# Attention groups started one step before the last one ends, and the correction row D of the next group moved to the maxima's banks

## Chip, core and metric

The kernel runs on one core of one Trainium2 chip. The metric is the device time of one execution in microseconds. The time before is the median of three executions, 1124.32 us (1123.53 to 1124.39).

## The reference, cut to what is computed

```python
xn = _layernorm(x)                       # x: (2, 1024, 512)
qkv = clip(xn @ Wqkv.T, -8, 8)           # q, k, v; q and k then get a layer norm with weights
scores = einsum('bqhd,bkhd->bhqk', q, k) * 16 ** -0.5      # 32 heads of 16
scores = scores + slopes[None, :, None, None] * rel         # ALiBi
scores = where(causal, scores, -1e30)
out = einsum('bhqk,bkhd->bqhd', softmax(scores), v) @ Wout.T
g = silu(ffn(xn))                        # gated FFN with 4-bit weights, inner size 1792
return x + out * g
```

## The kernel before

There are three stages. The first (to about 186 us in the profile) makes q, k and v, splits q and k into three bf16 parts each and writes them to HBM as `stk`. The second (to about 714 us), the one that is changed, is attention. The third is the FFN and the output.

The second stage works on 16 **groups** (NG = 16, index i): 2 batches times 8 groups of 4 heads (GH = 4). A group has 1024 queries and 1024 keys. It is done in 12 **steps** (NSTEP = 12, index e): a step takes one half of the queries (512) against one tile of 128 keys, eight steps for the upper half of the queries and then four (FIRST = 8) for the lower half. In a step

- `second(i, s, e, p)`, p = 0 and 1, computes on TensorE the scores of two heads into the PSUM tile `pair[p]`, on the diagonal with two more matmuls that add the mask (`behind`). It waits until the exponential has read that pair (`exp_done`);
- ScalarE takes the exponential of each pair, 128x1024 where the step is full, into `pr` (`exps`);
- `pv(i, s, e-1)` multiplies the exponentials of the step before with the values into `bank[3]` (`b_o`).

No maximum is subtracted in ScalarE. The row maximum comes in as rows of the operand: **D0** (lower half of the queries) and **D1** (upper half) are the negated maxima, split into three bf16 parts by five small operations on GpSimd (`chain`), transposed on TensorE (`trans_d`), copied to SBUF (`dt_sb`) and written by a 12 KB DMA from ScalarE's queue (`send_d`) into rows 108 to 110 of the operand `qs`. The first scores of group i+1 wait for D1's DMA (`d1_in`).

The maxima need the scores in the other orientation. These **pieces** (query tile, head, first key, width; 48 in a group) go through a ring of three PSUM banks `b_m`: TensorE fills a bank (`score`), VectorE reads its maximum (`take`; with the causal mask and one more small instruction where the piece ends on the diagonal, `tensor_reduce` where not) and frees it (`m_free`). A piece waits until the one three places before it is read. In group i the pieces of query tiles 2 and 3 are the group's own (`OWN`), all others belong to group i+1. `plan` says which pieces stand after which of the 36 **places** (step e, parts 0, 1, 2: after `second(…, 0)`, after `second(…, 1)`, after `pv`). The ring also carries the outputs: `copy_o` (ScalarE) copies `b_o` to `ot`, `trans_o` transposes it in four matmuls, VectorE divides (`normalise`); O1 is the upper half of the queries, O0 the lower.

At the end of a group the order before is: D1's transpose into `pair[0]` after step 10, ScalarE's copy of it, step 11's scores, `pv` of step 10, four pieces, `pv` of step 11, two pieces, O0, and then the next group.

SP's queue loads the operands of group i+2 in two halves of 14 or 15 DMAs (`load(..., 1)` after `pv` of step 7, `load(..., 0)` with the values after `pv` of step 11), and before them 4-bit weights for the third stage (`half_job`: `zst` and `sst`, 448 KB each), which ScalarE converts (`convert`, two instructions) and GpSimd subtracts (`job`). Three such jobs lie in two groups.

Of the kernel before, what the change touches and what calls it, by code (L numbers as in the profile page):

```python
# [18 lines left out]

# [7 lines left out]
BF16 = mybir.dt.bfloat16  # L27
# [31 lines left out]
def build(nc, x, wproj, lnw, w_all, z_all, s_all, ident_in, identb_in, tri_in, behind_in, qrows, krows, out):  # L59
# [7 lines left out]
    with ExitStack() as ctx:  # L67
# [142 lines left out]
        LATER_KEYS = len(EARLY) // 2  # L210

        PLACES = 3 * NSTEP
        OWN_END = 8
        LOW_AT = 15
        EARLY_END = 28
        TAIL = 6
        BEFORE = 4
        D0_AT, D1_AT, O1_AT = 5, 10, 9
        JOB_AT = 6

        def spread(lot, lo, hi):

            width = [w for e in range(NSTEP) for w in (512 - STEPS[e][2], 512 - STEPS[e][2], 512 - STEPS[e - 1][2])]
            total, work = sum(width[lo:hi]), sum(pc[3] + 60 for pc in lot)
            out, at, passed = {h: [] for h in range(PLACES)}, 0, 0
            for h in range(lo, hi):
                passed += width[h]
                while at < len(lot) and (h == hi - 1 or sum(pc[3] + 60 for pc in lot[:at]) < work * passed / total):
                    out[h].append(lot[at])
                    at += 1  # L230
            return out
        parts_of_plan = (spread(LATE[HEAD:], 0, OWN_END), spread(EARLY[:LATER_KEYS], OWN_END - 1, LOW_AT),
                         spread(EARLY[LATER_KEYS:], LOW_AT, EARLY_END), spread(LATE[:HEAD - TAIL], EARLY_END, PLACES))
        plan = {h: sum((part[h] for part in parts_of_plan), []) for h in range(PLACES)}
        plan[3 * D0_AT + 2].append("D0")
        plan[3 * O1_AT + 2].append("O1")
        tail = LATE[HEAD - TAIL:HEAD] + ["O0"]

        own = [x for h in range(PLACES) for x in plan[h] if x in LATE[HEAD:] or isinstance(x, str)] + ["O0"]
        order = [x for h in range(PLACES) for x in plan[h]] + tail  # L240
        RING = len(order)
        assert RING % 3 == 0
        HEAD_ORDER = LATE[:HEAD // 2] + EARLY + LATE[HEAD // 2:HEAD]
        PREP = len(HEAD_ORDER)
        number = ({x: n for n, x in enumerate(order)}, {x: n for n, x in enumerate(own)})

        def at(x, last):

            return number[last is True][x]

        def ring_bank(x, last):
            return b_m[(PREP + at(x, last)) % 3]

        def base(i):

            return PREP + RING * i

# [527 lines left out]
        USES = (NSTEP + 1, NSTEP)  # L785
        D1_USE = D1_AT + 1
# [3 lines left out]
        def full(i, e, p, last):  # L790

            return USES[p] * i + e + 1 + (1 + (e > D1_AT and not last) if p == 0 else 0)

        def full_d1(i):

            return USES[0] * i + D1_USE + 2

# [5 lines left out]
        with nc.Block() as block:  # L803
            @block.sync
            def _(sp):
# [16 lines left out]
                def body(i, s, ip, last):  # L822
# [20 lines left out]
            def _(pool):  # L843
# [16 lines left out]
                def body(i, s, ip, last):  # L860

                    pool.wait_ge(m_free, base(i) + at(LATE[-1], last) + 1)
                    pool.wait_ge(s_full[0], USES[0] * i + 1)
                    chain(pool, mx0[:, :, :], 2 * i + 1)
                    job(ip, (0, 2)[s])
                    if not last:

                        pool.wait_ge(mx1_done, i + 2)

                        pool.wait_ge(m_full, base(i) + at("D0", last) + 1)  # L870
                        chain(pool, mx1[:, 0, :, :], 2 * i + 2)
# [823 lines left out]
```

## Time and profile before

| | |
|---|---|
| median of three executions | 1124.32 us |
| the profiled execution's own time | 1123.91 us |
| its span, first to last instruction | 1121.8 us |
| mean granted TensorE clock | 0.993 of full speed |
| busy share of the span, TensorE / VectorE / ScalarE / GpSimd | 93% / 83% / 65% / 41% |
| second stage, groups 1 to 14, 226.22 to 685.79 us | 459.57 us, of which TensorE busy 433.28 |

A busy TensorE is not one at its peak: the records of matmuls overlap, and a short wait can hide in them. In the timelines below the start times are therefore what is read: what lies between the starts of two rows is what the first took, waits included.

### The profile page before, as it was taken

Reading aid. Unit: us, or ns where it says so; the run is one execution under the profiler, and the core shown is the slowest. Engines: PE = TensorE matmul, PEld = TensorE weight load, DVE = VectorE, ACT = ScalarE, POOL = GpSimd, SP = SyncE. Lnnn points to the kernel's source line nnn. Section 1 sums busy time; section 2 is a strip of 40 time slices with the busy share of each in tenths; the row PEclk is TensorE's granted clock in tenths of the full one; section 3 lists DMA queues with packets and bytes.
Section 4 is the critical chain, followed back from the end, with each engine's and each line's share of the span. In section 5 each row is a group of like instructions: output and inputs, shape, how many; then the busy total and the mean of one; then the engine's idle time right before and its main releaser. Section 6 shows DMA issues by size and latency. Waiting matters only on the chain. (4 is left out here: it accounts for less than half of the span.)

```text
span 1121.8 us, 18965 instructions
## 1 busy us (share of the span) xinstructions
PE 1043.7 (93%) x6242; PEld 635.6 (57%) x6242; DVE 926.4 (83%) x2147; ACT 725.7 (65%) x1167; POOL 465.1 (41%) x554
## 2 busy tenths in 40 slices
PE   5999987999999999999999999899999999999995
PEld 4788764333333433333333333487778778777874
DVE  6788897787878888788888875579989998998896
ACT  3666565676667667666666667567747766774774
POOL 2666645111111111111111111039946864994786
PEclk9999998999999999999999999999999999999998
DMA  6254753453543334454343433100120011012001
GB/s 212 77 155 142 214 144 94 133 119 72 142 108 95 113 100 119 75 142 109 89 120 96 120 77 105 39 1 0 39 70 7 1 55 59 1 39 75 1 1 38
DMA packets 98584, 95.32 MB, mean 85 GB/s; under 512 B 28030, under 2 KB 80950, under 8 KB 98486
## 3 DMA queue, kind: packets, MB, share of 16 engines
q1 hardware_dynamic: 96854, 93.72, 29.9%
q8 instruction: 50, 0.82, 0.3%
q10 hardware_dynamic: 1632, 0.39, 0.2%
q14 instruction: 48, 0.39, 0.1%
HBM read 72.45 MB, written 21.23 MB: 84 GB/s over the span
## 5 line engine op out<-in xcount | busy, mean ns | idle before, releaser
L883 ACT ACTIVATE pr<-pair 128x1024 f32<-128x1024 f32 (+3 forms) x384 | 293.1, 811 | 151.2 <-PE pair L999 97.0
L266 DVE CUSTOM_DVE_ANT_0 bank<-bank,sg 128x384 f32<-128x384 f32 (+1 forms) x488 | 227.5, 521 | 65.6 <-PE bank L276 62.1
L1527 PE MATMUL pair<-xc_lo,w_gu 128*128 128x512 f32 x448 | 181.5, 405 | 4.5 <-DVE xc_lo L1363 4.5
L1528 PE MATMUL pair<-xc_hi,w_gu 128*128 128x512 f32 x448 | 175.3, 391 | 0.0
L269 DVE TENSOR_REDUCE mx<-bank 128x1 f32<-128x512 f32 x240 | 150.1, 682 | 8.9 <-PE bank L276 8.2
L1375 DVE SCALAR_TENSOR_TENSOR gate<-pair,sgu,gate 128x512 f32<-128x512 f32 x168 | 124.5, 741 | 25.7 <-PE pair L1528 24.1
L1166 POOL TENSOR_TENSOR yt<-yt,tmp 128x512 f32<-128x512 f32 x96 | 124.2, 1314 | 0.0
L276 PE MATMUL bank<-ks,qs 108*128 108x512 bf16 (+3 forms) x384 | 107.7, 329 | 5.3 <-DVE mx L266 5.1
L1527 PEld LDWEIGHTS pair<-xc_lo,w_gu 128*128 128x128 f32 x448 | 84.1, 188 | 37.3 <-DVE up L1375 6.6
L1156 POOL TENSOR_TENSOR h_lo<-gate,h_hi 128x512 fp32r<-128x512 f32 x56 | 72.5, 1296 | 76.6 <-ACT h_hi L1209 76.6
L994 PE MATMUL pair<-s_sb,xin_c 111*128 111x512 bf16 (+3 forms) x384 | 95.1, 332 | 7.7 <-ACT dt L395 2.9
L276 PE MATMUL bank<-xin_c,s_sb 108*128 108x512 bf16 (+3 forms) x344 | 98.0, 334 | 4.4 <-DVE mx L266 4.1
L994 PE MATMUL pair<-qs,ks 111*128 111x512 bf16 (+3 forms) x384 | 93.1, 327 | 7.5 <-ACT pr L883 4.7
L1540 PE MATMUL bank<-h_lo,w_d 128*128 128x512 f32 x224 | 89.7, 400 | 2.9 <-POOL h_lo L1156 2.2
L1528 PEld LDWEIGHTS pair<-xc_hi,w_gu 128*128 128x128 f32 x448 | 84.3, 188 | 13.6
L371 POOL TENSOR_SCALAR dneg<-mx 128x16 f32<-128x16 f32 x32 | 8.2, 255 | 198.0 <-DVE mx L266 113.2
L850 POOL TENSOR_TENSOR w_gu<-sst,zst 128x896 fp32r<-128x896 f32 x16 | 33.4, 2085 | 135.5 <-ACT zst L896 135.5
L1541 PE MATMUL bank<-h_hi,w_d 128*128 128x512 f32 x224 | 88.2, 394 | 0.0
L709 PE MATMUL bank<-wq_hi,xt_lo 128*128 128x512 f32 x192 | 79.4, 413 | 5.4 <-DVE xt_lo L597 5.4
L1241 ACT ACTIVATE gate<-gate 128x512 f32<-128x512 f32 x56 | 35.4, 632 | 73.2 <-DVE gate L1375 73.2
L1166 POOL TENSOR_TENSOR yt<-yt,oin_v 128x512 f32<-128x512 f32 x48 | 65.3, 1360 | 37.9 <-ACT oin_v L1263 37.5
L1009 PE MATMUL bank<-pr,oin_v 128*17 128x512 f32 (+3 forms) x768 | 80.8, 492 | 0.0
(125 smaller groups left out, 2121.4 us busy)
## 6 DMA issues: line engine op xcount, KB each, us to landing
stk<-parts SPq DMA_DIRECT2D x16, 768.0 KB, 5.7
zst<-in_z_all SPq DMA_DIRECT2D x24, 448.0 KB, 4.0
sst<-in_w_all SPq DMA_DIRECT2D x24, 448.0 KB, 4.7
xin_c<-in_x SPq DMA_DIRECT2D x32, 256.0 KB, 3.3
s_sb<-stk SPq DMA_DIRECT2D x96, 64.0 KB
xin_c<-stk SPq DMA_DIRECT2D x96, 64.0 KB
qs<-stk SPq DMA_DIRECT2D x96, 64.0 KB
ks<-stk SPq DMA_DIRECT2D x96, 64.0 KB
```

What stands on the lines that cost most here:

```text
L266: dve.tensor_tensor_reduce(out=src, in0=src, in1=tri[:, 512 - w:512], scale=1.0, scalar=-3.0e38, op0=ALU.add, op1=ALU.max, accum_out=dst). ...
L269: dve.tensor_reduce(dst, src, AX.X, ALU.max).then_inc(m_free, 1)
L276: pe.matmul(b[:, 0:w], qs[s][0:ROWS_MAX, qt // 4, j, (qt % 4) * P:(qt % 4 + 1) * P], ks[s][0:ROWS_MAX, j, k0:k0 + w], start=True, stop=Tru ...
L883: act.activation(pr[e % 3][:, 2 * p:2 * p + 2, 0:w], pair[p][:, :, 0:w], ACT.Exp, scale=SCALE)\
L994: mm = pe.matmul(pair[p][:, jj, 0:512 - c0], ks[s][0:ROWS, j, kt * P:(kt + 1) * P], qs[s][0:ROWS, qb, j, c0:512], start=True, stop=not dia ...
L1009: mm = pe.matmul(b_o[32 * j:32 * j + VW, c0:512], vs[s][:, kt, j * VW:(j + 1) * VW], pr[e % 3][:, j, 0:512 - c0], start=(kt == 0), stop=(k ...
L1166: pool.tensor_tensor(yt[t][:, :], yt[t][:, :], tmp[n % 3], ALU.add).then_inc(dn_pool, 1)
L1375: dve.scalar_tensor_tensor(out=a, in0=GB[j % 4], scalar=scale_of(n, k, it), in1=a, op0=ALU.mult, op1=ALU.add)\
L1527: pe.matmul(GB[j % 4], w, xc_lo[:, k, :], start=True, stop=False)
L1528: pe.matmul(GB[j % 4], w, xc_hi[:, k, :], start=False, stop=True).then_inc(gu_done, 1)
L1540: pe.matmul(y[t][:, :], w_down(it, t), h_lo[n % 4][:, :], start=True, stop=False)
L1541: pe.matmul(y[t][:, :], w_down(it, t), h_hi[n % 4][:, :], start=False, stop=True).then_inc(dn_done, 1)
```

## The change

The scores keep their places and their order; the plan is now written out as a table of 36 places. What differs in the second stage:

- `pv` of step 11 and O0 of group i move into group i+1: `pv` to step 0 (part 2), O0 to step 1 (part 1). All six last pieces stand together at the end of the group. `copy_o(i, 1)` follows the exponentials of step 0 of group i+1.
- D1 is transposed into a ring bank and copied by VectorE; before, it went into `pair[0]` and was copied by ScalarE, and step 11 waited for the copy.
- `second` of a group's first step now waits for the exponentials of the last step of the group before.
- On SP, `load(..., 1)` waits for the scores of step 7 and not for `pv` of step 7; `load(..., 0)` for the scores of step 11, and the values' DMA alone for `pv` of step 11.
- The job that stood at the end of an even group (`convert(ip, 1)`) comes before the exponentials of step 2 of the odd one.

```diff
+        PLAN = (
+            "2 2", "2", "",
+            "2 3", "O0 3", "3",
...
+            "7", "0", "O1",
+            "", "0", "D1",
+            "", "", "0 0 1 1 1 1",
+        )
...
-                        sp.wait_ge(pv_done, PV0 + NSTEP * i + FIRST)
+                        sp.wait_ge(s_full[1], full(i, FIRST - 1, 1))
                         load(sp, i + 2, s, 1)
 
+                        sp.wait_ge(s_full[1], full(i, NSTEP - 1, 1))
+                        load(sp, i + 2, s, 0, values=False)
+
                         sp.wait_ge(pv_done, PV0 + NSTEP * i + NSTEP)
-                        load(sp, i + 2, s, 0)
+                        load_v(sp, i + 2, s)
...
-                        if e == D1_AT + 1 and not last:
-                            send_d1(act, 1 - s, full_d1(i), i + 2, pair[0][:, 0, :])
+                        if e == place_of["D1"] + 1 and not last:
+
+                            act.wait_ge(m_free, number(i, "D1") + 1)
+                            send_d(act, 1 - s, 1, d1_in)
+                        if e == JOB1_AT and s == 1:
+                            convert(ip, 1)
...
+                        exps(i, e, 0)
+                        exps(i, e, 1)
+                        if e == 0 and i > 0:
+                            copy_o(i - 1, 1)
+                        if e == FIRST:
                             copy_o(i, 0)
...
+                    if x in ("D0", "D1"):
+                        dve.wait_ge(m_full, n + 1)
+                        dve.tensor_copy(dt_sb[int(x[1])][:, :], ring_bank(i, x)[0:48, 0:P // 2].bitcast(BF16)).then_inc(m_free, 1)
...
+                    if i > 0 or e > 0:
+
+                        pe.wait_ge(exp_done, 2 * NSTEP * i + 2 * e - 1 + p)
...
-                            if h == 3 * e + 2 and e > 0:
+                            if part == 2 and e > 0:
                                 pv(i, s, e - 1)
...
-                        if e == NSTEP - 1:
-                            ring(i, s, tail[:BEFORE], last)
-                        if e == D1_AT and not last:
-
-                            pe.wait_ge(exp_done, 2 * NSTEP * i + 2 * e + 1)
-                            trans_d(pe, 2 * i + 2, pair[0][:, 0, :], s_full[0])
-                    pv(i, s, NSTEP - 1)
-                    ring(i, s, tail[BEFORE:], last)
+                            elif part == 2 and i > 0:
+                                pv(i - 1, 1 - s, NSTEP - 1)
+                            for x in plan[3 * e + part]:
+                                if present(x, i):
+                                    fill(i, s, x)
```

Below is TensorE's order at D1, in the first group (slot 0, operands `s_sb` and `xin_c`), before the change. `d3` is the split maximum, `identb` the identity, `pair` the score tiles, `bank3` the output's accumulator.

```order
L384 MATMUL pair0<-identb,d3 48x128 [waits d_chain,exp_done]
L994 MATMUL pair0<-s_sb,xin_c 128x128 [waits d_copied]
L994 MATMUL pair0<-s_sb,xin_c 128x128
L999 MATMUL pair0<-behind,identb 128x128 x2
L994 MATMUL pair1<-s_sb,xin_c 128x128 [waits exp_done]
L994 MATMUL pair1<-s_sb,xin_c 128x128
L999 MATMUL pair1<-behind,identb 128x128 x2
```

And with the change:

```order
L397 MATMUL bank0<-identb,d3 48x128 [waits d_chain,m_free]
L1012 MATMUL pair0<-s_sb,xin_c 128x128 [waits exp_done]
L1012 MATMUL pair0<-s_sb,xin_c 128x128
L1017 MATMUL pair0<-behind,identb 128x128 x2
L1012 MATMUL pair1<-s_sb,xin_c 128x128 [waits exp_done]
L1012 MATMUL pair1<-s_sb,xin_c 128x128
L1017 MATMUL pair1<-behind,identb 128x128 x2
```

D1 now goes into a ring bank and waits for the ring (`m_free`), and step 11's first scores wait for an exponential and no longer for the copy of D1. The second place is the end of the group on TensorE, from the fourth of the six last pieces to the first scores of the next group (`qs1`, `ks1`), before:

```order
L276 MATMUL bank0<-ks1,qs1 128x256 [waits m_free]
L1009 MATMUL bank3<-pr2,oin_v 17x128 [waits exp_done]
L1009 MATMUL bank3<-pr2,oin_v 17x128 x3
L276 MATMUL bank1<-ks1,qs1 128x256 [waits m_free]
L276 MATMUL bank2<-ks1,qs1 128x256 [waits m_free]
L1018 MATMUL bank0<-ident,ot 128x128 [waits ot_done,m_free]
L1018 MATMUL bank0<-ident,ot 128x128 x3
L994 MATMUL pair0<-qs1,ks1 128x512 [waits d1_in]
L994 MATMUL pair0<-qs1,ks1 128x512
```

With the change, from the same piece to `pv` of step 11:

```order
L289 MATMUL bank1<-ks1,qs1 128x256 [waits m_free]
L289 MATMUL bank2<-ks1,qs1 128x256 [waits m_free]
L289 MATMUL bank0<-ks1,qs1 128x256 [waits m_free]
L1012 MATMUL pair0<-qs1,ks1 128x512 [waits exp_done,d1_in]
L1012 MATMUL pair0<-qs1,ks1 128x512
L289 MATMUL bank1<-ks1,qs1 128x384 [waits m_free]
L289 MATMUL bank2<-ks1,qs1 128x384 [waits m_free]
L1012 MATMUL pair1<-qs1,ks1 128x512 [waits exp_done]
L1012 MATMUL pair1<-qs1,ks1 128x512
L289 MATMUL bank0<-ks1,qs1 128x384 [waits m_free]
L1027 MATMUL bank3<-pr2,oin_v 17x128 [waits exp_done]
L1027 MATMUL bank3<-pr2,oin_v 17x128 x3
```

The `pv` of 17x128 (step 11's) and the transposes of `ot` have left the way to the first scores; the `pv` stands now behind the third piece of step 0, and O0 (not shown) behind the second scores of step 1. On ScalarE the same stretch reads before:

```order
L395 ACTIVATE dt1<-pair0 48x128 [waits s_full0]
L389 DMA qs1<-dt1 3x16x128 [waits d_copied]
L883 ACTIVATE pr2<-pair0 128x2x128 [waits pv_done,s_full0]
L883 ACTIVATE pr2<-pair1 128x2x128 [waits pv_done,s_full1]
L890 ACTIVATE ot<-bank3 128x512 [waits pv_done]
L895 ACTIVATE sst<-sst 128x896 [waits z_in]
L896 ACTIVATE zst<-zst 128x896
```

and with the change:

```order
L402 DMA qs1<-dt1 3x16x128 [waits m_free]
L896 ACTIVATE pr2<-pair0 128x2x128 [waits pv_done,s_full0]
L896 ACTIVATE pr2<-pair1 128x2x128 [waits pv_done,s_full1]
L896 ACTIVATE pr0<-pair0 128x1024 [waits pv_done,s_full0]
L896 ACTIVATE pr0<-pair1 128x1024 [waits pv_done,s_full1]
L903 ACTIVATE ot<-bank3 128x512 [waits pv_done]
L896 ACTIVATE pr1<-pair0 128x1024 [waits pv_done,s_full0]
```

The copy of D1 is gone from ScalarE, its DMA waits for VectorE (`m_free`), and the copy of the output stands behind the exponentials of the next group's first step.

## Rows read from the trace of the kernel before

**Rows 1.** Busy time by engine in stretches: one group, and the sum of groups 1 to 14.
```profile
391.00:423.54 32.54, 30.87 (x236) 12.59 (x234) 26.71 (x86) 21.75 (x30) 4.26 (x11) 1.00 0.37 96
...
sum 459.57, PE 433.28 PEld 175.98 DVE 374.69 ACT 306.79 POOL 74.16; mean PE 30.95 PEld 12.57 DVE 26.76 ACT 21.91 POOL 5.30
```
**Rows 2.** Waits, 226 to 686 us: us in total, times, longest.
```profile
PE pair L994 <- ACT dt L395: 5.1, 14, 0.4
...
PEld pair L994 <- DMA s_sb<-dt: 1.4, 3, 0.9
...
PEld pair L994 <- DMA qs<-dt: 0.6, 2, 0.3
```
**Rows 3.** Timeline of TensorE around the starts of groups 4 (325.56) and 7 (423.54).
```profile
325.56 0.61 PE L994 MATMUL pair<-s_sb,xin_c 111*128 111x512 bf16 x2 [0.66 <-DMA s_sb<-dt]
...
419.25 0.24 PE L384 MATMUL pair<-identb,d 128*48 128x128 bf16 x1
...
421.85 0.41 PE L1009 MATMUL bank<-pr,oin_v 128*17 128x128 f32 x8
422.20 0.39 PE L276 MATMUL bank<-ks,qs 108*128 108x256 bf16 x2
423.07 0.63 PE L1018 MATMUL bank<-ident,ot 128*128 128x128 f32 x4 [0.49 <-DVE mx L266]
423.54 0.60 PE L994 MATMUL pair<-qs,ks 111*128 111x512 bf16 x2
...
425.58 0.60 PE L994 MATMUL pair<-qs,ks 111*128 111x512 bf16 x2 [0.52 <-ACT pr L883]
...
428.89 0.38 PE L276 MATMUL bank<-ks,qs 108*128 108x512 bf16 x1
...
430.83 1.05 PE L1009 MATMUL bank<-pr,vs 128*17 128x512 f32 x8
```
**Rows 4.** Timeline of ScalarE at the same two starts; ACTq is its queue.
```profile
321.01 0.73 ACTq L389 DMA_DIRECT2D s_sb<-dt  x1
...
419.82 0.73 ACTq L389 DMA_DIRECT2D qs<-dt  x1
...
422.33 0.60 ACT L890 ACTIVATE ot<-bank 128x512 f32<-128x512 f32 x1 [1.03 <-PE bank L1009]
...
424.51 3.75 ACT L883 ACTIVATE pr<-pair 128x1024 f32<-128x1024 f32 x4
```
**Rows 5.** Timeline of VectorE in the first steps of group 7.
```profile
423.74 0.26 DVE L929 RECIPROCAL rec<-bank 128x16 f32<-128x16 f32 x1 [0.35 <-PE bank L1018]
...
424.38 0.56 DVE L266 CUSTOM_DVE_ANT_0 bank<-bank,sg 128x384 f32<-128x384 f32 x1
...
429.31 0.70 DVE L266 CUSTOM_DVE_ANT_0 bank<-bank,sg 128x512 f32<-128x512 f32 x1
```
**Rows 6.** Timeline of TensorE in the first steps of group 6, an even one.
```profile
391.00 0.60 PE L994 MATMUL pair<-s_sb,xin_c 111*128 111x512 bf16 x2
...
392.71 0.60 PE L994 MATMUL pair<-s_sb,xin_c 111*128 111x512 bf16 x2 [0.19 <-ACT pr L883]
...
397.97 1.05 PE L1009 MATMUL bank<-pr,oin_v 128*17 128x512 f32 x8
```
**Rows 7.** Timeline of SP's queue in group 7.
```profile
415.05 0.33 SPq L180 DMA_DIRECT2D s_sb<-stk  x1
...
422.55 0.82 SPq L180 DMA_DIRECT2D s_sb<-stk  x1
...
444.11 0.33 SPq L811 DMA_DIRECT2D zst<-in_z_all  x1
...
447.92 0.33 SPq L180 DMA_DIRECT2D qs<-stk  x1
```
**Rows 8.** The page's DMA issues: KB each, median us from issue to landing.
```profile
sst<-in_w_all SPq DMA_DIRECT2D x24, 448.0 KB, 4.7
...
out<-s_sb SPq DMA_DIRECT2D x16, 256.0 KB, 2.5
```

More of the change, by code:

```diff
@@ L20 @@
+from collections import Counter
 from contextlib import ExitStack
@@ L209, in build @@
         HEAD = 8
[L210 to L239, printed above, removed]
@@ L240, in build @@
-        order = [x for h in range(PLACES) for x in plan[h]] + tail
-        RING = len(order)
-        assert RING % 3 == 0
+        OWN = LATE[HEAD:]
         HEAD_ORDER = LATE[:HEAD // 2] + EARLY + LATE[HEAD // 2:HEAD]
         PREP = len(HEAD_ORDER)
[L245 to L256, printed above, removed]
+        PLACES = 3 * NSTEP
@@ new lines, in build @@
+        plan = [[item(token) for token in row.split()] for row in PLAN]
+        in_order = [x for row in plan for x in row]
+        assert sorted(x for x in in_order if not isinstance(x, str)) == sorted(EARLY + LATE)
+        place_of = {x: h // 3 for h, row in enumerate(plan) for x in row}
+        of_kind = {name: [x for x in in_order if x in lot] for name, lot in
+                   (("own", OWN), ("early", EARLY), ("head", LATE[:HEAD]),
+                    ("upper", [x for x in EARLY if x[2]]), ("lower", [x for x in EARLY + LATE[:HEAD] if not x[2]]))}
@@ new lines, in build, with present, number @@
+        JOB_AT, JOB1_AT = 6, 2
+        def present(x, i):
+            if x == "O0":
+                return i > 0
+            if x in ("D0", "O1") or x in OWN:
+                return True
+            return i < NG - 1
+        ring_of = [[x for x in in_order if present(x, i)] for i in range(NG)]
+        ring_of[NG - 1].append("last O0")
+        place_in = [{x: n for n, x in enumerate(r)} for r in ring_of]
+        first_in = [PREP + sum(len(r) for r in ring_of[:i]) for i in range(NG)]
+        def number(i, x):
+            return first_in[i] + place_in[i][x]
@@ L258, in take, with ring_bank @@
+        def ring_bank(i, x):
+            return b_m[number(i, x) % 3]
         def take(dve, pc, b, n):
@@ L783, in w_half, with full @@
             return w_d[:, ip * HALF:(ip + 1) * HALF] if n == 2 else w_gu[:, (2 * ip + n) * HALF:(2 * ip + n + 1) * HALF]
-        USES = (NSTEP + 1, NSTEP)
-        D1_USE = D1_AT + 1
         EXTRA = 1
         PV0 = 3
[L790 to L796, printed above, removed]
+        def full(i, e, p):
+            return NSTEP * i + e + 1 + (p == 0)
         def groups(body):
@@ L981, in slot0_free, with fill @@
-                def slot0_free(i, e, last):
-                    if e == D1_AT + 1 and not last:
-                        pe.wait_ge(d_copied, i + 2)
-                    elif e > 0:
-                        pe.wait_ge(exp_done, 2 * NSTEP * i + 2 * e - 1)
+                def fill(i, s, x):
+                    n = number(i, x)
+                    if x in ("D0", "D1"):
+                        pe.wait_ge(m_free, n - 2)
+                        trans_d(pe, 2 * i + (1, 2)[int(x[1])], ring_bank(i, x), m_full)
+                    elif x == "O1":
+                        trans_o(i, 0, n)
+                    elif x == "O0":
+                        trans_o(i - 1, 1, n)
+                    elif x in OWN:
+                        score(pe, s, x, ring_bank(i, x), n)
+                    else:
+                        if x == of_kind["upper"][0]:
+                            pe.wait_ge(stk_in[1 - s][1], LOADS[1] * (i // 2 + 1 + s))
+                        if x == of_kind["lower"][0]:
+                            pe.wait_ge(stk_in[1 - s][0], LOADS[0] * (i // 2 + 1 + s))
+                        score(pe, 1 - s, x, ring_bank(i, x), n)
```

121 lines of the change are left out of this document (59 added, 62 removed).

## Prediction

> **What bounds the kernel now.** I read the busy time of stretches first. From the start of group 1 to the start of group 15, 14 groups take 459.6 us, 32.8 us each, and TensorE is busy in 31.0 of them, VectorE in 26.8, ScalarE in 21.9 [rows 1]. TensorE bounds the stage, but its records overlap, so the 1.8 us left is not all that it waits. I therefore went on to the timelines and read distances between starts. The end of a group is where the change works. The marks there are D1's transpose (419.25) and the first scores of the next group (423.54): 4.29 us apart [rows 3]. In them stand step 11's scores, `pv` of step 10, six pieces, `pv` of step 11 and O0. Two waits are seen: the wait for ScalarE's copy of D1, 5.1 us in 14 groups or 0.36 each [rows 2], and 0.49 before O0, which comes last there [rows 3].
>
> The row to look at next is one that does not look like a bound. D1's DMA is issued at 419.82 and the scores that need it start at 423.54, 3.72 later, and they are released by O0's transposes and not by the DMA [rows 3, 4]. But in group 4 the issue is at 321.01 and the start at 325.56, 4.55 later, and there it is the DMA that ends the wait, after 0.66 us [rows 3, 4]. The weight loads of such scores waited for D1's DMA in five of the 15 starts, 1.4 + 0.6 = 2.0 us in all [rows 2]. So the DMA's landing lies just below the work that covers it in ten starts, and above it in five. A mean start is thus 4.29 + 2.0/15 = 4.42 us behind D1.
>
> **The change, part by part.** I cut a period of 32.8 us into three stretches: D1 to the next group's first scores (a), these to `pv` of step 0 behind the four narrow pieces, which is step 2's last part (b), and the rest (c).
>
> *The rest (c)* keeps its instructions and their order: the pieces stand at the same places as before (the two orders of TensorE agree there piece by piece), so nothing is gained by the order of keys and width itself. D1's copy adds 0.2 us to VectorE where it is idle. Zero, while VectorE has 6 us of 32.8 free [rows 1].
>
> *Stretch (a), what TensorE has to do.* Before, the last pieces are issued by 422.20 + 0.39 = 422.59, which is 3.34 behind D1. Of that 0.36 (the copy of D1) and 0.35 (`pv` of step 11, 421.85 to 422.20) go [rows 2, 3]. TensorE is ready for the next group 2.6 us behind D1, where it was 4.29. If nothing else held it, 1.7 us would be won each time.
>
> *Stretch (a), what D1 needs.* The DMA is still issued 0.57 behind D1 (419.25 to 419.82): VectorE's copy takes the place of ScalarE's, and I add 0.01 for it, 0.58 [rows 3, 4]. Then it has to land, L, and 0.05 passes until the scores start (an estimate from the small distance at a semaphore). Neither end of L is shown directly, so I bound it. From below by the shortest landing of the page, 2.5 us for the output's stores, at a time with little other traffic [rows 8]. From above by group 4, 4.5 us [rows 3, 4]. Now L lies under 3.7 in ten starts and between 3.7 and 4.5 in five; I take its mean as 3.6. So with the change the first scores come max(2.6, 0.63 + L) behind D1, and since 0.63 + 2.5 is already 3.1, D1's DMA sets it in every case. The cover of 3.72 us that hid the landing is what the change takes away: the wait that goes at O0 comes back as a wait for `d1_in`.
>
> *What becomes of L.* It is longer than 2.5 because SP's loads are in flight. Before, the load of the second half starts at 415.05, 4.8 us before D1's DMA, and runs to 422.55, where the next load follows without a gap [rows 7]. With the change it starts when step 7's scores are done, which is about when SP has issued the two weight DMAs (444.11, and the second some 1.1 later), so at about 445.2 in place of 447.92 [rows 7]. Its 14 DMAs take 7.5 us (415.05 to 422.55), and D1's DMA at 452.7 comes just when they have been issued and the next load begins. That is for a smaller L. Against it: 0.9 MB of weights, which take 4.7 us to land [rows 8], now stand directly ahead of these loads, where 3.4 us lay between. I take 3.3.
>
> The Trainium skill ("DMA: Bandwidth & Descriptors", "Queues, rings and completion order") says that a DMA's semaphore increment is a strongly ordered write, which lands only after every earlier write of that DMA engine, across its queues. By it D1's landing hangs on what SP has in flight and not on D1's 12 KB, and stays slow as long as loads run beside it. Group 4 agrees with it but doesn't prove it.
>
> *Stretch (b).* It now holds `pv` of step 11 and O0 as well, 0.35 + 0.5 us of TensorE. Count from the first scores (0). The first exponential ends so that step 1's scores start at 1.71 in group 6, behind a seen wait of 0.19 [rows 6]; in group 7, where ScalarE converts weights first, at 2.04 [rows 3]. TensorE would be there at 1.36: the second scores start at 0.76 and take 0.44, the third piece some 0.16 (an estimate: 384 of 512 columns of the 0.22 below). `pv` of step 11, 0.35, fills this gap exactly: 1.71. Step 1's second scores follow at 2.63 (the second exponential, 3.75/4 later [rows 4]). Then ScalarE copies the output, 0.60 long [rows 4], so O0 starts at about 3.2. VectorE reads it 0.67 later (423.07 to 423.74) and goes on to a piece 1.31 behind O0's start [rows 3, 5], at 4.5. TensorE goes on at 3.7: a piece 0.22 (428.89 to the next scores), `pv` 0.99, a piece, scores 0.44; the fourth 512-wide piece is issued at 5.55 and read 0.42 later (428.89, 429.31), at 5.97 [rows 3, 5]. Before, that reading was 429.31 - 423.54 = 5.77 behind the first scores, and the `pv` that ends the stretch started 1.52 behind it, at 7.29 (430.83); in group 6 at 397.97 - 391.00 = 6.97 [rows 3, 5, 6]. With the change 5.97 + 1.52 = 7.49, against a mean of 7.13: +0.36.
>
> **The sum.** For a start with loads: 0.63 + L - 4.42 + 0.36 = L - 3.43. With L = 3.3, -0.13 us, in 14 starts -1.8. The 15th start (group 15) has no loads beside it: 0.63 + 2.5 - 4.29 + 0.36 = -0.8. Together -2.6 us. The profiled execution took 1123.91 us (span 1121.8), 0.4 under the median, so 1121.3 for it and 1121.7 for the median: -0.2%.
>
> **The rivals.**
> 1. *D1's DMA stays as slow as it is* (the skill's rule, with the loads beside it as before): L = 3.6 gives +0.17 x 14 - 0.8 = +1.6 us, 1125.9. For it: SP issues without a pause before and after. Chance 0.25.
> 2. *The landing gets worse*, the other side: the loads come directly behind 0.9 MB of weights, the queue is still full when D1's DMA is issued, and every start is like group 4's, L = 4.5: +1.07 x 14 - 0.8 = +14 us, 1138. It decides from L = 3.7 on. For it: such a start exists. Against: 7.5 us have passed since the weights' issue, and they take 4.7. Chance 0.22.
> 3. *D1's DMA meets a quiet moment*, L = 2.5: -0.93 x 14 - 0.8 = -14 us, 1110. For it: the gap between the two loads. Against: SP hardly pauses. Chance 0.20.
> 4. *The wait for D1 is no bound at all* and all of 1.7 - 0.36 = 1.3 us is won 15 times: -20 us, 1104. It needs a landing under 2.0 us, below any row. Chance 0.02.
>
> **How the numbers follow.** The forecast (L from 3.0 to 3.6, 1117 to 1126) has 0.31. My sum of stretch (b) may be off by 0.2 us a group, 3 us in all. The range runs from 1110 to 1134 (L = 2.5 to 4.2). A measurement of this kernel tells 0.2%, 2.2 us, from no change, so faster is under 1122.1: half of the forecast's case, all of 3 and 4, a part of 1, together 0.43; within 0.2% 0.29; slower, 2 and the rest of 1, 0.28.
>
> **What would show it.** In the profile after: the wait for the copy of D1 and the waits before O0 at the end of a group are gone; in their place the first scores of nearly every group wait for the DMA of `dt`, 0.5 to 1.5 us; D1 to the first scores takes 3.9 us (L = 3.3), and the first scores to the `pv` of step 0 7.5. ScalarE's conversion in step 2 costs nothing. The prediction is wrong if the first scores do not wait for `dt`, if L is under 3 or over 3.7, or if a wait for exponentials appears in steps 1 to 3 where ScalarE has the output's copy and the conversion.

## The result and the profile after

Over 20 executions of each kernel the median is 1131.51 us (1125.89 to 1143.0) against 1124.14 us (1123.11 to 1128.68): a ratio of 1.007, with a 95% interval of 1.0055 to 1.0085. The changed kernel is 0.7% slower, where 0.2% faster was forecast. The profiled execution took 1139.53 us, its span is 1137.7, so it is one of the longer ones of the 20. Its mean granted clock of TensorE is 0.977. In the others it lies between 0.971 (the two of 1142.03 and 1143.0 us) and 0.986 (one of them of 1127.49), always under the 0.993 of the profile before. The kernel before is not at 0.993 each time either: 22 more executions of it, taken beside the first experiments, have 0.986 to 0.994.

The page of the changed kernel: the span, the busy times by engine, and the granted clock in 40 slices.

```profile
span 1137.7 us, 18980 instructions
...
PE 1058.1 (93%) x6242; PEld 639.5 (56%) x6242; DVE 930.1 (82%) x2162; ACT 722.3 (63%) x1152; POOL 465.4 (41%) x554
...
PEclk9999999999999998999999999999999999999997
```

TensorE is busy 14 us longer than before (1043.7) at the same instructions. The waits of TensorE in the second stage (us in total, times, longest), to be laid beside [rows 2]:

```profile
PE pair L1012 <- DMA qs<-dt: 10.8, 7, 3.0
PE bank L289 <- DVE mx L279: 8.3, 28, 0.3
PE pair L1012 <- DMA s_sb<-dt: 7.5, 7, 1.9
```

The wait for ScalarE's copy is gone. In its place 14 of the 15 starts show a wait for D1's DMA, 18.3 us in all. The start of group 7 on TensorE, with [rows 3] beside it (columns as there: start, us, instructions, idle time before and what ended it):

```profile
425.85 0.24 PE L397 MATMUL bank<-identb,d 128*48 128x128 bf16 x1
...
427.81 0.91 PE L289 MATMUL bank<-ks,qs 108*128 108x256 bf16 x3 [0.29 <-DVE mx L279]
431.16 1.04 PE L1012 MATMUL pair<-qs,ks 111*128 111x512 bf16 x2 [2.43 <-DMA qs<-dt]
431.99 0.85 PE L289 MATMUL bank<-ks,qs 108*128 108x384 bf16 x2
432.62 1.06 PE L1012 MATMUL pair<-qs,ks 111*128 111x512 bf16 x2
433.48 0.53 PE L289 MATMUL bank<-ks,qs 108*128 108x384 bf16 x1
433.94 0.63 PE L1027 MATMUL bank<-pr,oin_v 128*17 128x128 f32 x8
434.50 1.03 PE L1012 MATMUL pair<-qs,ks 111*128 111x512 bf16 x2
...
436.67 0.60 PE L1038 MATMUL bank<-ident,ot 128*128 128x128 f32 x4
...
438.63 0.60 PE L1012 MATMUL pair<-qs,ks 111*128 111x512 bf16 x2
```

D1 at 425.85, the next group's first scores at 431.16: 5.31 us, before 4.29. The reader should then look at a column that the prediction never read, the duration: scores of the same shape take 0.60 us each in [rows 3], 1.04 to 1.06 here, and 0.60 again from 438.63 on. Group 11, some 140 us later, has the same rows with a shorter wait and the old durations:

```profile
568.83 0.61 PE L1012 MATMUL pair<-qs,ks 111*128 111x512 bf16 x2 [0.47 <-DMA qs<-dt]
...
569.60 0.60 PE L1012 MATMUL pair<-qs,ks 111*128 111x512 bf16 x2
...
570.29 0.41 PE L1027 MATMUL bank<-pr,oin_v 128*17 128x128 f32 x8
570.63 0.61 PE L1012 MATMUL pair<-qs,ks 111*128 111x512 bf16 x2
...
572.04 0.63 PE L1038 MATMUL bank<-ident,ot 128*128 128x128 f32 x4
...
576.41 0.62 PE L1027 MATMUL bank<-pr,vs 128*17 128x512 f32 x4
...
```

The windows tell why. First three short stretches around the start of group 7, then the whole groups 1, 7 and 11 (columns: from:to, length, busy time of PE, PEld, DVE, ACT, POOL, then the granted clock, the DMA share and GB/s; the full clock, 2.4 GHz, is 1.00, and 0.50 is the lower level, 1.2 GHz):

```profile
427.00:430.40 3.40, 1.34 (x10) 0.46 (x6) 2.13 (x12) 0.66 (x2) 0.00 (x0) 0.88 1.15 142
431.10:434.50 3.40, 3.34 (x16) 1.05 (x16) 1.60 (x5) 1.80 (x2) 0.00 (x0) 0.50 0.85 127
434.50:437.90 3.40, 3.40 (x23) 1.43 (x19) 2.00 (x8) 2.79 (x5) 0.00 (x0) 0.72 0.54 124
...
224.01:258.12 34.11, 32.41 (x234) 13.02 (x235) 27.09 (x87) 22.65 (x30) 6.30 (x12) 0.95 0.51 115
...
431.16:465.84 34.68, 33.28 (x234) 13.25 (x235) 26.99 (x87) 22.64 (x30) 6.30 (x12) 0.92 0.50 112
568.83:601.03 32.20, 31.02 (x234) 12.54 (x234) 27.01 (x88) 22.31 (x30) 6.32 (x12) 1.00 0.50 122
```

In the first steps of group 7 TensorE is granted half its clock, after it had done nothing from 428.72, where its last piece ends, to 431.16. Its busy time grows by 2.3 us from group 11 to group 7 at the same 234 matmuls.

The table has the distances of all starts, taken from the traces: L is D1's DMA from its issue to the last update of its semaphore; a, from D1's transpose to the next group's first scores; rest, from a group's first scores to its D1. "Low" marks the groups in whose first steps the granted clock is 0.50.

```
                  before                 after
group i    L    a    rest of i+1    L    a    rest of i+1   low
 0        3.57  4.30   28.57       3.33  3.90   30.26       x
 1        3.89  4.51   28.27       3.28  3.85   30.26       x
 2        3.47  4.30   28.57       3.34  3.91   30.26       x
 3        4.50  5.12   28.26       4.22  4.79   30.21       x
 4        3.12  4.30   28.58       3.43  4.00   30.17       x
 5        2.69  4.30   28.25       3.40  3.97   30.17       x
 6        3.35  4.30   28.57       4.74  5.31   31.13       x
 7        3.46  4.29   28.25       2.98  3.55   28.86
 8        3.94  4.56   28.32       5.33  5.90   30.25       x
 9        3.74  4.36   28.57       3.80  4.37   30.26       x
10        3.92  4.54   28.33       2.77  3.34   28.87
11        3.86  4.48   28.26       2.77  3.34   28.86
12        3.60  4.30   28.58       4.07  4.63   30.21       x
13        3.38  4.29   28.26       3.23  3.80   30.22       x
14        2.21  4.29               2.29  2.86
```

The sum of the 14 periods from group 1's start to group 15's went from 459.57 to 477.61, +18.0 us, in three parts: the distances a −4.3; the rest of the undisturbed groups from 28.40 to 28.86, 14 x 0.46 = +6.4; and the low clock, 1.3 to 1.4 us in ten groups and 2.3 in group 7 (31.13 − 28.86), together +15.9. Group 1 starts 2.2 us earlier (226.22 and 224.01), and what follows the start of group 15 takes 436.1 us, 436.0 before. +18.0 − 2.2 = +15.8, against 15.9 between the spans.

The 2.2 us are no gain of the change. They are the low clock too, but in the kernel before, in the first steps of its first group (the second row is the changed kernel's):

```profile
191.23 1.04 PE L994 MATMUL pair<-s_sb,xin_c 111*128 111x512 bf16 x2 [2.71 <-DVE bank L955]
...
191.62 0.61 PE L1012 MATMUL pair<-s_sb,xin_c 111*128 111x512 bf16 x2 [2.71 <-DVE bank L972]
```

Behind the same idle time of 2.71 us the granted clock from 191.2 to 197.2 is 0.50 in the profile before and 1.00 in the one after. From its first scores to D1 the group takes 30.69 us before and 28.49 after. Without the low clock in either kernel, the changed one would still be 6.4 − 4.3 = 2.1 us slower (an estimate from these parts).

### The profile page after: what moved, and what is told of

It is laid out like the page before. It is cut to its first block and busy times, and to the rows that moved or that the text cites. A ratio compares the mean times of both kernels' runs of the same rounds, so it can differ in the third digit from the quotient of the medians.

```text
span 1137.7 us, 18980 instructions
## 1 busy us (share of the span) xinstructions
PE 1058.1 (93%) x6242; PEld 639.5 (56%) x6242; DVE 930.1 (82%) x2162; ACT 722.3 (63%) x1152; POOL 465.4 (41%) x554
## 5 line engine op out<-in xcount | busy, mean ns | idle before, releaser
L896 ACT ACTIVATE pr<-pair 128x1024 f32<-128x1024 f32 (+3 forms) x384 | 296.4, 811 | 190.0 <-PE pair L1017 101.3
L289 PE MATMUL bank<-ks,qs 108*128 108x512 bf16 (+3 forms) x384 | 112.8, 341 | 5.8 <-DVE mx L279 4.7
L1012 PE MATMUL pair<-qs,ks 111*128 111x512 bf16 (+3 forms) x384 | 99.2, 344 | 12.9 <-DMA qs<-dt 10.8
L1012 PE MATMUL pair<-s_sb,xin_c 111*128 111x512 bf16 (+3 forms) x384 | 97.8, 340 | 10.4 <-DMA s_sb<-dt 7.5
L289 PE MATMUL bank<-xin_c,s_sb 108*128 108x512 bf16 (+3 forms) x344 | 100.8, 339 | 5.3 <-DVE mx L279 4.3
L1027 PE MATMUL bank<-pr,vs 128*17 128x512 f32 (+3 forms) x768 | 81.6, 498 | 0.0
```

The costliest lines, as they stand in the source:

```text
L289: pe.matmul(b[:, 0:w], qs[s][0:ROWS_MAX, qt // 4, j, (qt % 4) * P:(qt % 4 + 1) * P], ks[s][0:ROWS_MAX, j, k0:k0 + w], start=True, stop=Tru ...
L896: act.activation(pr[e % 3][:, 2 * p:2 * p + 2, 0:w], pair[p][:, :, 0:w], ACT.Exp, scale=SCALE)\
L1012: mm = pe.matmul(pair[p][:, jj, 0:512 - c0], ks[s][0:ROWS, j, kt * P:(kt + 1) * P], qs[s][0:ROWS, qb, j, c0:512], start=True, stop=not dia ...
L1027: mm = pe.matmul(b_o[32 * j:32 * j + VW, c0:512], vs[s][:, kt, j * VW:(j + 1) * VW], pr[e % 3][:, j, 0:512 - c0], start=(kt == 0), stop=(k ...
```

## The experiments

Each ratio is against executions of the kernel before that were taken beside the run (medians 1124.0 to 1124.8 us). Averages and counts of groups are, unless said otherwise, over the 13 starts of groups 2 to 14 in the profiled execution. By that count the changed kernel has L = 3.64, a = 4.21 and ten groups with the low clock; the one before has 3.61, 4.43 and none.

**Without the loads.** Both kernels without the loads of groups 2 to 15, which then work with the data of groups 0 and 1 (the values too); the waits of the pieces for these loads are lowered to match, and everything else is kept. In the changed kernel (in the one before, its two load lines):

```diff
-                        load(sp, i + 2, s, 1)
...
-                        load(sp, i + 2, s, 0, values=False)
...
-                        load_v(sp, i + 2, s)
```

> The changed kernel without SP's loads of the operands of groups 2 to 15 (these groups then work on the data of groups 0 and 1; the weight DMAs stay). Theory A (D1's DMA lands late because SP's loads are in flight, that sets each group's start, and the wait lets TensorE's clock fall): D1's DMA lands in 2.2 to 2.3 us, the first scores come 2.9 us behind D1, the granted clock stays full in the stage, and the time is 1107 to 1111 us. Theory B (the stretch behind the start is what costs, by O0 and the later pieces, and the DMA is hidden): the time falls by no more than that of the kernel before without the loads, 1129 or more.

Measured: 1106.77 us (1105.96 to 1110.0), 0.9845 of the kernel before (0.9813 to 0.9877).

> The kernel before without SP's loads of the operands of groups 2 to 15 (same omission). Theory A: D1's DMA was hidden in ten of 15 starts, so only the late ones shrink to 4.29 us, -2 us in all: 1122. Theory B: the same, 1122 to 1124.

Measured: 1123.32 us (1120.63 to 1126.66), ratio 0.9987 (0.997 to 1.0005): no difference.

Two groups of the changed kernel without loads:

```profile
224.82:256.46 31.64, 30.91 (x235) 12.45 (x235) 26.91 (x88) 22.31 (x30) 6.31 (x12) 1.00 0.17 60
414.68:446.34 31.66, 30.93 (x236) 12.45 (x235) 26.93 (x90) 22.31 (x30) 6.31 (x12) 1.00 0.20 60
```

The starts of groups 1 to 15 now come 2.76 to 2.82 us behind D1, with landings of 2.2 us, and the granted clock is 1.00 in groups 1 to 14. In the kernel before, the landing falls to the same 2.2 us and the starts stay at 4.29 to 4.30: there the work in stretch (a) covers it. So the change does free 1.5 us a start (1106.77 against 1123.32 us where neither kernel has loads), and the landing of a 12 KB DMA beside the loads takes most of it back (a is 4.21 with them).

**The clock by itself.** Four matmuls of 512 columns that write into a ring bank whose next user overwrites them, between the last piece and the wait for `d1_in`. They add work and take no wait away.

```diff
+                        if e == 0 and i > 0:
+                            n = number(i, in_order[0])
+                            pe.wait_ge(m_free, n - 2)
+                            for _ in range(4):
+                                pe.matmul(b_m[n % 3][:, 0:512], ks[s][0:ROWS_MAX, 0, 0:P], qs[s][0:ROWS_MAX, 0, 0, 0:512], start=True, stop=True)
                         if e == 0:
                             pe.wait_ge(d1_in, 16 * i + 16)
```

> The changed kernel with four matmuls more per group (108x512 scores of the group's own, written to the ring bank that is filled next and overwritten there), between the last piece and the wait for D1's DMA: 0.86 us more of TensorE work where it would sit idle. Theory A (the idle time lowers the granted clock for the first steps of the group, which costs 1.4 us each time): no stretch at the lower clock at the starts of groups, 1124 to 1128 us, faster than the changed kernel though it does more. Theory B (the clock falls for another reason): 1131 or more.

Measured: 1128.62 us (1125.0 to 1134.68), ratio 1.0034 (1.0014 to 1.0053); the profiled span is 1123.5 us at a mean clock of 0.996. The start of a group, and the waits that are left:

```profile
389.86 1.04 PE L1050 MATMUL bank<-s_sb,xin_c 108*128 108x512 bf16 x4
390.73 0.60 PE L1012 MATMUL pair<-s_sb,xin_c 111*128 111x512 bf16 x2
...
391.50 0.59 PE L1012 MATMUL pair<-s_sb,xin_c 111*128 111x512 bf16 x2
```
```profile
PE pair L1012 <- DMA qs<-dt: 1.8, 2, 0.9
PE pair L1012 <- DMA s_sb<-dt: 0.2, 1, 0.2
```

The matmuls fill most of the time until the DMA lands, the scores behind them take 0.60 us, and no group of this execution has the low clock; a is 4.08 and the rest 28.86 on average. 14 us of span are back at the same instructions plus 60. The landings of this execution were shorter too (L = 3.20 on average), so part of the gain in a is theirs; the rest, 28.86 in every group, shows the clock by itself. Not every execution is as good (the median's is 3 us above the profiled one), but half of the loss goes with matmuls that compute nothing.

**The landing, by what SP has in flight.** The second load starts only when D1's DMA has landed:

```diff
                         sp.wait_ge(s_full[1], full(i, NSTEP - 1, 1))
+                        sp.wait_ge(d1_in, 16 * i + 32)
                         load(sp, i + 2, s, 0, values=False)
```

> The changed kernel, but SP's second load of a group waits until D1's DMA has landed. Theory A1 (what D1's landing waits for includes the loads issued behind it): it lands in 2.5 to 3.0 us in place of 3.6, the clock falls in few groups, 1112 to 1120 us. Theory A2 (it waits for what was issued ahead of it alone): it lands in 3.2 to 3.6 us, 1128 to 1132.

Measured: 1118.26 us (1116.11 to 1121.79), ratio 0.9946 (0.9926 to 0.9966). SP's queue between the two loads, with a gap from 417.96 to 420.74 where [rows 7] have none:

```profile
417.10 0.86 SPq L185 DMA_DIRECT2D xin_c<-in_krows  x1
420.74 0.33 SPq L181 DMA_DIRECT2D s_sb<-stk  x1
```

Issue to start falls from 3.69 to 3.00 on average (2.53 to 3.64), a to 3.52, and one group of 13 has the low clock. So the landing depends on the loads issued behind D1's DMA as well. The first load and the weights before it still stand ahead of D1's DMA; without any load issue to start is 2.26.

**The loads' waits alone, in both kernels.** The changed kernel with the waits of before, and the kernel before with the new ones:

```diff
-                        sp.wait_ge(s_full[1], full(i, FIRST - 1, 1))
+                        sp.wait_ge(pv_done, PV0 + NSTEP * i + FIRST)
                         load(sp, i + 2, s, 1)
-                        sp.wait_ge(s_full[1], full(i, NSTEP - 1, 1))
-                        load(sp, i + 2, s, 0, values=False)
                         sp.wait_ge(pv_done, PV0 + NSTEP * i + NSTEP)
-                        load_v(sp, i + 2, s)
+                        load(sp, i + 2, s, 0)
```

> The changed kernel with SP's loads back where they were (behind pv of step 7 and behind pv of step 11, values with the second). Theory A (the cover of D1's DMA is gone, and where the loads start makes no difference to its landing, 3.6 us in both): landing 3.5 to 3.8 us, time as the changed kernel's, 1128 to 1134 us. Theory C (the earlier loads, directly behind the weights, are what made the starts late): landings spread less and the time falls to 1120 to 1126.

Measured: 1139.49 us (1133.23 to 1146.9), ratio 1.0136 (1.009 to 1.0183). The expected 1128 to 1134 was missed. The landing is 3.5 on average, a 4.09, both a little under the changed kernel's, and 11 of 13 groups have the low clock. The profiled execution (1140.47) is as long as the changed kernel's (1139.53), so the trace does not show where the 8 us between the medians lie.

> The kernel before with only SP's loads started as in the changed one. Theory A: D1's DMA is covered for 3.72 us; a landing of 3.6 us in the mean with single ones over 4 costs 1 to 3 us in all, 1124 to 1127. Theory C: 1130 or more.

Measured: 1123.28 us (1121.58 to 1126.77), ratio 0.9993 (0.9982 to 1.0004). The landing falls from 3.6 to 3.1 on average, and a from 4.43 to 4.34 only. Next to nothing comes of it, because stretch (a) has 3.72 us of cover. The earlier loads are thus no part of the loss; they are harmless before and, by the medians, help after.

**D1 one place up**, so that the same cover stands behind an earlier issue:

```diff
-            "", "0", "D1",
+            "", "0 D1", "",
```

> The changed kernel with D1 transposed before pv of step 9 and not after it (one place earlier). Theory A: the DMA is issued about 0.5 us earlier against the rest of the group (ScalarE is busy with step 10 until then), the wait shrinks by that, and the clock falls in fewer groups: 1114 to 1124 us. Rival: GpSimd's split of the maxima is not ready so early, TensorE waits for it, and nothing is won: 1131.

Measured: 1123.58 us (1119.2 to 1132.22), ratio 0.9999 (0.9973 to 1.0025). The chain was ready in time. a is 4.22, counted from the earlier D1, and the rest is 28.1 in groups at the full clock: 32.3 us together, where the changed kernel has 4.21 + 28.86 = 33.1. Four of 13 groups have the low clock. That is a gain of 8 us on the changed kernel and none on the one before.

> Both: D1 one place earlier, and SP's second load behind D1's landing. Theory A: the two add, landing 2.9 us, start of the next group 0.5 us earlier than with the late load alone: 1109 to 1114 us. Rival: D1's DMA, issued earlier, stands deeper in the first load and lands 0.5 us later: 1116 to 1119.

Measured: 1116.97 us (1113.98 to 1122.79), ratio 0.9938 (0.9916 to 0.9959). That is 1.3 us under the late load alone, with intervals that overlap, so no difference is shown. The two gains do not add: issue to start is 3.48 here and 3.00 there. A reason would be that D1's DMA now goes out while more of the first load is in flight; no run separates it.

**An idle moment in the kernel before, first attempt.** D1 is sent behind step 11's exponentials instead of ahead of them.

```diff
...
+                    if not last:
+                        act.wait_ge(d_copied, i + 2)
+                        send_d(act, 1 - s, 1, d1_in)
```

> The kernel before, with D1's DMA issued on ScalarE behind the exponentials of step 11 (its copy stays where it was): about 1.5 us later, 2.1 us behind D1's transpose. No work is moved on TensorE. Theory A: with 3.6 us to land the first scores come 5.75 us behind D1 in place of 4.42, +1.3 us a group or +19 in 14; and the idle time of about 1.5 us lowers the clock, +1.4 us a group or +20: 1155 to 1165 us, with stretches at the lower clock at the starts of groups. Theory B (the lower clock belongs to something else of the changed kernel): 1143.

Measured: 1126.61 us (1124.28 to 1127.93), ratio 1.002 (1.0011 to 1.003). 1155 to 1165 was expected from an issue 1.5 us later. The issue moved by 0.70 us only, from 0.57 to 1.27 behind D1, and the landing was shorter (issue to start 3.27), so a is 4.54, TensorE is idle for 0.45 us at the most, and no group has the low clock. It tells nothing of the clock, since there was no longer wait to test it with.

**`pv` of step 11 back at the end of its own group**, in the changed kernel:

```diff
-                            elif part == 2 and i > 0:
-                                pv(i - 1, 1 - s, NSTEP - 1)
...
+                    pv(i, s, NSTEP - 1)
```

> The changed kernel with pv of step 11 back at the end of its own group; O0 stays in the next. TensorE then works 0.35 us of the wait for D1's DMA, and step 1's first scores wait for the exponential where the pv was. Theory A: the starts stay where they are, the wait is 0.35 us shorter, and the clock falls in fewer groups: 1124 to 1130 us. Rival: pv waits for the exponentials of step 11 and costs 0.3 us a group: 1131 to 1136.

Measured: 1127.8 us (1122.84 to 1132.46), ratio 1.0036 (1.0018 to 1.0055). The undisturbed rest stays 28.86, the shortest a is 3.16, and three of 13 groups have the low clock. `pv` costs nothing while TensorE waits for the DMA anyway and keeps it at work: the half of the overlap that moved it gained nothing.

**The weights late too.** Beside the late second load, the weights' DMAs that stood ahead of the first load go behind D1's landing; ScalarE converts them a step later.

```diff
-        JOB_AT, JOB1_AT = 6, 2
+        JOB_AT, JOB1_AT = 6, 3
...
-                    if not last:
+                    if not last and last is not None:
                         half_job(*((ip, 1), (ip + 1, 0))[s])
-                    else:
+                    elif last:
...
                         sp.wait_ge(s_full[1], full(i, FIRST - 1, 1))
                         load(sp, i + 2, s, 1)
 
+                        sp.wait_ge(d1_in, 16 * i + 32)
+                        half_job(*((ip, 1), (ip + 1, 0))[s])
                         sp.wait_ge(s_full[1], full(i, NSTEP - 1, 1))
                         load(sp, i + 2, s, 0, values=False)
```

> As the kernel with the second load behind D1's landing, and the weight DMAs that stood ahead of the first load moved behind that landing too (the conversion that follows first one step later). Theory A: the first load starts 1 us earlier and on free queues, D1's DMA lands in 2.3 to 2.7 us, 1108 to 1113 us. Rival: the second load comes 1 us later behind 0.9 MB and TensorE waits for it in step 5, or ScalarE for the weights in step 3: 1118 or more.

Measured: 1112.03 us (1110.84 to 1115.34), ratio 0.9899 (0.9881 to 0.9917), the shortest of all runs that keep their loads. SP and TensorE at the start of group 7, and two groups:

```profile
411.84 0.86 SPq L185 DMA_DIRECT2D xin_c<-in_krows  x1
415.41 0.37 SPq L818 DMA_DIRECT2D zst<-in_z_all  x1
```
```profile
412.58 0.24 PE L397 MATMUL bank<-identb,d 128*48 128x128 bf16 x1
...
415.44 0.60 PE L1014 MATMUL pair<-qs,ks 111*128 111x512 bf16 x2
```
```profile
225.07:257.04 31.97, 31.02 (x235) 12.46 (x235) 27.25 (x90) 22.42 (x30) 6.34 (x12) 1.00 0.60 125
415.44:447.08 31.64, 30.91 (x236) 12.53 (x235) 26.91 (x88) 22.44 (x30) 6.33 (x12) 1.00 0.52 126
```

SP issues nothing from 412.70 to 415.41, D1's DMA lands in that gap, issue to start is 2.40 on average (2.23 to 2.91), and at 415.44 the start comes 2.86 behind D1 and without an idle row. a is 2.92 on average, the rest 28.87, the clock 1.00. 14 x (2.92 + 28.87 − 32.83) = −14.6 us, and the 14 periods take 444.97, which is 14.6 less than before. The span is 11.0 less, because 4.7 us are lost behind the start of group 15 (440.7 us to the end, 436.0 before). There SP issues the last weights at 681.67 only, ScalarE waits for them, and TensorE for ScalarE:

```profile
687.34 0.95 ACT L910 ACTIVATE sst<-sst 128x896 f32<-128x896 int32 x1 [2.17 <-DMA sst<-in_w_all]
...
689.67 0.39 PE L1014 MATMUL pair<-qs,ks 111*128 111x128 bf16 x2 [2.92 <-ACT pr L898]
```

> The two together. Theory A: as with the weights late, within 2 us, since without a fallen clock it does not matter where pv of step 11 stands: 1107 to 1114.

Measured: 1116.52 us (1115.5 to 1118.35), ratio 0.9936 (0.9921 to 0.9951), 4.5 us slower than without `pv` there and outside the 1107 to 1114 expected. Once the DMA lands early, `pv` is what sets the start: a is 3.15 at the least. So the overlap is worth something, but only behind a fast landing.

**An idle moment in the kernel before, second attempt.** D1's DMA goes out behind ScalarE's copy of the output (its old place is taken out, as in the first attempt), then the same with nine matmuls of 512 columns in the place of the wait:

```diff
...
                     copy_o(i, 1)
+                    if not last:
+                        act.wait_ge(ot_done, EXTRA + 2 * i + 2)
+                        act.wait_ge(d_copied, i + 2)
+                        send_d(act, 1 - s, 1, d1_in)
```

> The kernel before with D1's DMA issued behind ScalarE's copy of the output, about 3.7 us behind D1's transpose in place of 0.57. The first scores then come 7.1 us behind D1 (landing 3.3), 2.7 us later than before, and TensorE is idle for that. Theory A (idle time lowers the clock): +2.7 x 15 = 40 us and in addition about 1.4 us a group at the lower clock, 1180 to 1190 us. Theory B (the clock falls by something of the changed order): 1160 to 1168 and the clock stays full.

Measured: 1184.93 us (1184.49 to 1190.14), ratio 1.053 (1.0505 to 1.0554). A start, and the windows around it:

```profile
418.01 1.03 PE L999 MATMUL pair<-s_sb,xin_c 111*128 111x512 bf16 x2 [2.53 <-DMA s_sb<-dt]
...
419.48 1.06 PE L999 MATMUL pair<-s_sb,xin_c 111*128 111x512 bf16 x2
...
424.91 0.60 PE L999 MATMUL pair<-s_sb,xin_c 111*128 111x512 bf16 x2
```
```profile
414.00:417.40 3.40, 0.99 (x10) 0.55 (x6) 1.85 (x8) 0.60 (x1) 0.00 (x0) 0.94 0.51 116
418.00:421.40 3.40, 3.39 (x9) 1.34 (x10) 1.65 (x6) 1.85 (x2) 0.00 (x0) 0.50 0.67 131
```

> The same with nine matmuls of 108x512 (1.9 us at the full clock) between the transposes of O0 and the wait for D1's DMA. Theory A: no fall of the clock at the starts, 1160 to 1168 us, faster than without them. Theory B: as without them.

Measured: 1157.18 us (1156.27 to 1159.59), ratio 1.0289 (1.0262 to 1.0316). A fourth execution took 5503.53 us; it is left out, and why it did is not known. A start of this one:

```profile
475.07 0.59 PE L999 MATMUL pair<-s_sb,xin_c 111*128 111x512 bf16 x2
...
476.03 0.60 PE L999 MATMUL pair<-s_sb,xin_c 111*128 111x512 bf16 x2 [0.19 <-ACT pr L884]
...
478.90 0.60 PE L999 MATMUL pair<-s_sb,xin_c 111*128 111x512 bf16 x2
```

Here the edits of the pair of kernels differ in nothing but idle or filled time: a is 6.79 and 6.64, the rest 30.49 and 28.29. With the wait all 13 groups have the low clock, the same 0.50 as in the changed kernel; filled, none, and the time is 27.8 us shorter at 135 matmuls more. So the order of work that the change brings is not needed for the low clock; the kernel before has it at every start once TensorE is idle there for 1.5 to 2.8 us.

## Why the prediction was wrong

The forecast was 0.2% faster, and the kernel became 0.7% slower; the time lies inside the range of 1110 to 1134 us, on the other side of the time before.

**What was right.** The bound that it named: D1's DMA sets every start, 0.05 us behind the landing, and the waits at the copy and at O0 at the end of a group are gone. Its issue, 0.58 behind D1 (0.52 measured). Stretch (b): 7.49 us forecast, 7.58 in group 11 (568.83 to 576.41) and in the other groups at the full clock, so +0.36 became +0.45. The conversion in step 2 and the order of the pieces cost and gain nothing. The start without loads (2.5 taken, 2.29 measured) and the L of before (3.6 taken as a mean, 3.61 measured; six of the 15 starts hung on it, not five).

**The first step that failed is the term L.** "I take 3.3": it was 3.62 on average over the 14 starts with loads (2.77 to 5.33), as before the change. In the sum it is worth 14 x 0.32 = +4.5 us. The argument for it was the place of the DMA between two loads. By the issues it does lie there (SP issues the first load's last DMA at 425.41 in group 6, D1's goes out at 426.37, the second load begins at 426.67), but the first load's semaphore is still being updated until 430.67, so both loads are in flight beside it. Rival 1, to which 0.25 was given, has the size right (3.6). The rule of the Trainium skill behind it ("DMA: Bandwidth & Descriptors", "Queues, rings and completion order": a completion is written only after the earlier writes of that DMA engine, across its queues) agrees with what the loads show: L is 2.2 us without them, 2.3 with 2.7 us of quiet on SP, 3.0 with the weights ahead, 3.6 with everything. Rival 1's sum gives 1125.9. The trace records the packets of ScalarE's queue, and they split L (averages of 14 starts, us):

```
                     issue to first packet   packets   last packet to landing   L
no loads                     1.37              0.27            0.57            2.21
before                       1.40              0.51            1.70            3.61
changed                      1.66              0.64            1.32            3.62
weights late too             1.41              0.27            0.67            2.34
```

Of the 1.40 us that the loads add before the change, 1.13 lie behind the DMA's own last packet and 0.03 ahead of its first; of the 1.41 in the changed kernel, 0.75 and 0.29. A queue in front of the DMA's packets is thus the smaller part, and more than half of the delay is where the rule of the Trainium skill puts it. Which other writes a landing waited for is not shown.

**The second, and the larger, is a term that the sum doesn't have.** Its stretches add durations read at 0.60 us for a pair of scores, as if a wait cost its own length. It costs more: 11 of the 14 groups have half the clock in their first steps, behind starts that left TensorE idle for 0.9 to 3.0 us (a less the 2.87 at which the last piece ends, 428.72 − 425.85), and lose 1.4 us each, one of them 2.3: 15.9 us of the profiled execution. The three at the full clock came after 0.5 to 0.7 us. Less the 2.2 us that the kernel before lost to the same clock in its first group, that is 13.7 of the 15.8 us; the other 2.1 (−4.3 + 6.4) are the terms that the sum does have, with L = 3.62, near rival 1's +1.6. At the starts of groups 1 to 15 the longest wait for D1 before the change was 0.66 us [rows 3]. But the 0.993 in the table of the profile before was never asked what it hung on, and the row at 191.23 above, 1.04 us for two scores behind 2.71 us of idle time, would have told. The filled kernels show this cause from both sides: in the profiled execution of the changed kernel with four matmuls more no group has the low clock, and the nine in the kernel before take back 27.8 us of 60.5. The Trainium skill ("TensorE: Matmul & The Clock Gate", "A second HAM failure mode: psum-queue depth-cycling") tells of a kernel in which short idle times between groups of matmuls send the clock back and forth between its two levels. The trace agrees (0.50 in 431.10:434.50, 1.00 over group 11), and a rival for the idle time that stretch (a) gained should have come of it.

**The rival on the slow side** (L = 4.5, 1138) ended near the profiled time for the wrong reason: L over 4 occurs in four of 14 loaded starts, not in all. Over all executions the loss is 7.4 us and not the 15.6 of the profiled pair. The granted clock goes with the time, 0.983 to 0.986 in the four shortest and 0.971 in the two longest, but no other execution has a trace, so the split between landing and clock is shown for one alone. What makes a landing 2.8 in one group and 5.3 in another is open.

## What to carry to other kernels

Work that stands between an issue and its landing is cover: before moving it away, measure what the landing takes beside the queue's other traffic, and give the small DMA a quiet queue first (here −12 us against the kernel before, where the same move without it is +7). Price a new wait on TensorE with the durations at the lower clock for the steps behind it, and look for it in the mean duration of one shape; matmuls on a bank that is overwritten anyway are a cheap test of whether a loss is idle time or clock.

## What the runs showed of the hardware

- After an idle stretch of 2.4 us between two groups, in an engine busy 93% of the time (the changed kernel), the granted clock was 0.50 and a pair of scores took 1.04 to 1.06 us in place of 0.60, for the first 5 us of the group (0.76 at 436.07). The length of the wait alone does not decide it: with D1 one place up, a start 4.90 us behind D1 (idle for 1.25) went on at the full clock and one 4.50 behind it (0.85) at half, and behind the same 2.71 us at the first group the clock was 0.50 in one profile and 1.00 in the other.
- The landing of a 12 KB DMA from ScalarE's queue: 2.2 us with nothing from SP, 3.6 on average and up to 5.33 beside 64 KB loads that SP issues every 0.47 us. More than half of what the loads add comes after the DMA's own last packet: 1.32 to 1.70 us on average, 0.57 without loads. The waiting scores start 0.05 us behind the landing.
